# A context vector added to y as it is read from PSUM, and an MLP run earlier in a convolution kernel

## The reference

```python
def _L0_cond_ref(x, c, weight, c_weight, bias):
    out = lax.conv_general_dilated(x, weight, window_strides=(1,), padding=[(4, 4)],
        dimension_numbers=('NCH', 'OIH', 'NCH'), feature_group_count=4)
    ctx = jnp.einsum('nd,od->no', c, c_weight)
    return out + ctx[:, :, None] + bias[None, :, None]
def _L1_cond_ref(x, embedding, W0, b0, W1, b1, W2, b2, weight, bias_k):
    h = jax.nn.gelu(embedding @ W0 + b0, approximate=False)
    h = jax.nn.gelu(h @ W1 + b1, approximate=False)
    att = jax.nn.softmax(h @ W2 + b2, axis=-1)
    agg_w = jnp.einsum('bk,koi->boi', att, weight[..., 0])
    return jnp.einsum('boi,bih->boh', agg_w, x) + (att @ bias_k)[:, :, None]
x = x + _L0_cond_ref(x, cond_128, L0_cond_weight, L0_cond_c_weight, fside_S_0)
x = x + _L1_cond_ref(x, cond_128, ...)
```

## Time and profile before

| | us |
|---|---|
| median of 3 runs (723.7 to 725.74) | 723.83 |
| the profiled execution | 723.61 |
| its span | 721.8 |
| busy: PE, PEld | 712.1, 701.6 |
| busy: DVE, ACT, POOL | 636.0, 602.8, 38.4 |
| DMA, mean | 246 GB/s |

### The profile page before, as it was taken

One profiled execution on the slowest core, in us unless ns is written; L12 is line 12 of the kernel. 1 busy time (PEld: TensorE's weight loads), 2 busy tenths in 40 slices (PEclk: granted clock), 3 DMA queues, 4 the chain that ended last, 5 costly groups with the idle time before them and its releaser, 6 DMA issues.

```text
span 721.8 us, 29496 instructions
## 1 busy us (share of the span) xinstructions
PE 712.1 (99%) x12419; PEld 701.6 (97%) x12419; DVE 636.0 (88%) x1145; ACT 602.8 (84%) x456; POOL 38.4 (5%) x43
## 2 busy tenths in 40 slices
PE   8999999999999999999999999999999999999996
PEld 6899999999999999999999999999999999999995
DVE  6999889889889989889889898998899898898983
ACT  5989888898888898898898898898898898898833
POOL 2890000000000000000000000000000000000000
PEclk9999999999999999999999999999999999999999
DMA  6447778778778678778778778778778778787657
GB/s 225 156 159 258 269 246 276 259 255 270 236 253 283 216 259 275 217 259 269 247 252 270 232 256 254 249 260 255 237 270 261 232 270 257 234 271 243 199 210 241
DMA packets 66551, 177.56 MB, mean 246 GB/s; under 512 B 7437, under 2 KB 50008, under 8 KB 50264
## 3 DMA queue, kind: packets, MB, share of 16 engines
q1 hardware_dynamic: 57218, 112.96, 51.1%
q10 hardware_dynamic: 9302, 64.14, 23.4%
HBM read 101.57 MB, written 75.50 MB: 245 GB/s over the span
## 4 chain that ended last, share of the span: by engine, by line
PE 96%; DMA 2%; DVE 1%; ACT 0%; SPq 0%; issue 0%; DVEq 0%; ACTq 0%
PE ps L451 72%; PE ps L482 24%; DMA x_in<-in_x_dram 1%; DMA mix_dram<-mix_parts 1%; DMA mix_rep<-mix_dram 0%; DVE y_lo L648 0%; PE ps L415 0%; SPq L305 0%; ACT x_hi L534 0%; DVE mix_odd L749 0%; PE ps L404 0%; PE ps L392 0%; DVE mix_even L749 0%; DVE x_in L793 0%; DVEq L72 0%
## 5 line engine op out<-in xcount | busy, mean ns | idle before, releaser
L451 PE MATMUL ps<-x_hi,cw_hi 32*128 32x512 f32 x3072 | 428.6, 385 | 0.4 <-ACT x_hi L534 0.4
L451 PE MATMUL ps<-x_hi,cw_lo 32*128 32x512 f32 x3072 | 428.0, 384 | 0.0
L530 ACT ACTIVATE x_ph<-x_in 128x2560 f32<-128x2560 f32 x63 | 322.2, 5116 | 1.8 <-DVE x_lo L637 1.8
L451 PEld LDWEIGHTS ps<-x_hi,cw_hi 32*128 32x128 f32 x3072 | 317.4, 183 | 2.2 <-issue 0.8
L451 PEld LDWEIGHTS ps<-x_hi,cw_lo 32*128 32x128 f32 x3072 | 317.2, 183 | 0.9 <-issue 0.2
L451 PE MATMUL ps<-x_lo,cw_hi 32*128 32x512 f32 x3072 | 284.9, 384 | 0.0
L451 PEld LDWEIGHTS ps<-x_lo,cw_hi 32*128 32x128 f32 x3072 | 253.2, 183 | 1.7 <-issue 0.8
L482 PE MATMUL ps<-y_hi,mix_rep 32*128 32x512 f32 x2048 | 225.0, 384 | 1.4 <-DMA mix_rep<-mix_dram 1.4
L556 ACT ACTIVATE z_out<-ps,par 128x1024 f32<-128x1024 f32 x124 | 144.3, 1223 | 72.4 <-PE ps L482 57.2
L648 DVE TENSOR_TENSOR y_lo<-ps,y_hi 128x512 fp32r<-128x512 f32 x256 | 158.9, 682 | 47.0 <-ACT y_hi L543 46.9
L482 PEld LDWEIGHTS ps<-y_hi,mix_rep 32*128 32x128 f32 x2048 | 195.1, 183 | 2.5 <-DMA mix_rep<-mix_dram 1.8
(11 more groups left out here) (88 smaller groups left out, 116.3 us busy)
## 6 DMA issues: line engine op xcount, KB each, us to landing
x_in<-in_x_dram SPq DMA_DIRECT2D x64, 1024.0 KB, 7.7
out_dram<-z_out ACTq DMA_DIRECT2D x61, 1024.0 KB, 7.8
mix_rep<-mix_dram SPq DMA_DIRECT2D x256, 128.0 KB, 2.7
mix_dram<-mix_parts SPq DMA_DIRECT2D x64, 128.0 KB, 4.2
out_dram<-z_out SPq DMA_DIRECT2D x2, 1024.0 KB, 3.9
out_dram<-x_in SPq DMA_DIRECT2D x2, 512.0 KB, 3.5
z_out<-in_L_cond_weight_dram SPq DMA_DIRECT2D x1, 512.0 KB, 3.9
cw_nat<-in_L_cond_weight_dram SPq DMA_DIRECT2D x1, 144.0 KB, 2.3
```

Source lines behind the costliest of these rows:

```text
L451: mm = pe.matmul(y_at(s)[:, g, :], w[rows, m, :], x_at(xx[buf(s)], rows, m), start=i == 0, stop=i == CONV - 1)
L530: nc.scalar.activation(x_ph[buf(s)][:, :, :, :], by_lane(x_in[buf(s)]), ACT.Copy).then_inc(x_split_ph, 1)
```

## The change

The context is added to y when it is read. `ctx_all` [128, 64, 4] holds, for each sample and group, the context's 32 values repeated on all four row groups; `spread_context` makes it with four products (`to_rows`, four identities side by side, built by VectorE at the start), in place of the eight of `context_mixed`. For each sample VectorE copies four columns of it to `ctx_now`; `y_hi` becomes an activation Identity with a column bias, and `y_lo` becomes (y + column) - `y_hi` in one three-operand instruction. `finish_table` has two instructions instead of three.

The small network is moved forward: w0 is issued ahead of b0 and b1, the first layer stands ahead of the convolution, second and third layer at steps 6 and 12, the transpositions at 14. Phases 0 and 1 of sample 0 are VectorE's, 2 and 3 ScalarE's, phase 3 behind the first GELU. On VectorE the softmax stands ahead of the second half of x_lo.

At the end, each row group of samples 62 and 63 waits for its own copy (`mix_late`), and SP issues the copies of 62 ahead of the store of 63.

```diff
@@ -157,7 +157,9 @@
 ctx_c = sb("ctx_c", [P, NS])
-agg_b = sb("agg_b", [P, NS])
+ctx_all = sb("ctx_all", [P, NS, G])
+ctx_now = [sb(f"ctx_now{k}", [P, G]) for k in range(U)]
+to_rows = sb("to_rows", [P, PH, Q])
@@ -227,6 +232,10 @@
     return isinstance(s[0], int) and number(s) == b
+def is_late(s):
+    return is_sample(s, NS - 2) or is_sample(s, NS - 1)
@@ -303,7 +312,8 @@
             sp.dma_start(rep_at(s)[Q * r:Q * r + Q, :, :, :].bitcast(F32).rearrange("c g h o -> c g (h o)"),
-                         mix_dram[b].rearrange("(g c) h o -> c g (h o)", g=G)).then_inc(mix_loaded[b], DMA)
+                         mix_dram[b].rearrange("(g c) h o -> c g (h o)", g=G)
+                         ).then_inc(mix_late[b][r] if is_late(s) else mix_loaded[b], DMA)
@@ -328,8 +338,8 @@
         if is_sample(s, NS - 1):
+            load_mix(after(s, -1))
             store_mix(s)
-            load_mix(after(s, -1))
@@ -375,7 +385,7 @@
         pe.wait_ge(first_loaded, DMA)
-        pe.wait_ge(cond_copied, 2)
+        pe.wait_ge(cond_copied, 1)
@@ -408,14 +418,18 @@
         pe.matmul(ps[:, 4, 0:NS], ctxw_t[:, :], cond_t[:, :], start=True, stop=True).then_inc(ctx_mm, 1)
-    def context_mixed():
+    def spread_context():
...
         pe.wait_ge(ctx_made, 1)
-        for k in range(NK):
-            mm = pe.matmul(ps[:, 6, k * NS:(k + 1) * NS], mixw_t[:, k, :], ctx_c[:, :], start=True, stop=True)
-        mm.then_inc(ctx_mix_mm, 1)
-
-    between = {16: first_layer, 18: second_layer, 20: third_layer, 21: turn_mixw, 24: context, 26: attention, 31: context_mixed}
+        pe.wait_ge(table_made, 1)
+        pe.wait_ge(rows_made, G)
+        for g in range(G):
+            rows = slice(Q * g, Q * g + Q)
+            mm = pe.matmul(ps[:, 4 + g, 0:NS], to_rows[rows, :, :].rearrange("c r o -> c (r o)"), ctx_c[rows, :],
+                           start=True, stop=True)
+        mm.then_inc(ctx_spread, 1)
+    between = {6: second_layer, 12: third_layer, 14: turn_mixw, 24: context, 27: attention, 31: spread_context}
@@ -425,7 +439,7 @@
                 if is_sample(s, 0):
-                    pe.wait_ge(x_phase_by_act, 1)
+                    pe.wait_ge(x_phase_by_dve, 1)
@@ -437,9 +451,9 @@
         if g == 0 and i == 4 and is_sample(s, 0):
-            pe.wait_ge(x_phase_by_dve, 1)
+            pe.wait_ge(x_phase_by_dve, 2)
         if g == 0 and i == 8 and is_sample(s, 0):
-            pe.wait_ge(x_phase_by_act, 2)
+            pe.wait_ge(x_phase_by_act, 1)
@@ -459,7 +473,9 @@
         if i == 0:
-            if r == 0:
+            if is_late(s):
+                pe.wait_ge(mix_late[buf(s)][r], DMA)
+            elif r == 0:
@@ -511,10 +527,12 @@
     pe.wait_ge(cond_loaded, DMA)
-    pe.transpose(ps[:, 4, 0:NS], cond_nat[:, :], ident[0:NS, 0:NS])
+    pe.transpose(ps[:, 4, 0:NS], cond_nat[:, :], ident[0:NS, 0:NS]).then_inc(cond_turned, 1)
+    keep_warm(1)
+    first_layer()
...
     pe.transpose(ps[:, 4, P:P + 3], bias_rows[:, :], ident[0:3, 0:3]).then_inc(cond_turned, 1)
-    keep_warm(3)
+    keep_warm(1)
@@ -540,7 +558,9 @@
             at_least(act, z_ready, done(s, PH, lag=-U))
-        nc.scalar.activation(y_hi[s[1]][:, g, :], y_at(s)[:, g, :], ACT.Copy).then_inc(y_hi_made, 1)
+            act.wait_ge(ctx_now_made, done(s))
+        nc.scalar.activation(y_hi[s[1]][:, g, :], y_at(s)[:, g, :], ACT.Identity,
+                             bias=ctx_now[s[1]][:, g:g + 1]).then_inc(y_hi_made, 1)
@@ -571,9 +591,9 @@
         (cond_nat[:, :], cond[:, :], cond_loaded),
+        (w0_sb[:, :], w0[:, :], first_loaded),
...
         (bias_rows[2:3, :], b1.rearrange("(a c) -> a c", a=1), biases_loaded),
-        (w0_sb[:, :], w0[:, :], first_loaded),
@@ -586,11 +606,11 @@
     act.wait_ge(x_loaded[0], DMA)
-    round_phase(0).then_inc(x_phase_by_act, 1)
...
     nc.scalar.activation(h1[:, :], ps[:, 5, 0:NS], ACT.Gelu, bias=cols[:, 1:2]).then_inc(mlp_act, 1)
+    round_phase(3).then_inc(x_hi_made, 1)
@@ -645,11 +665,25 @@
             at_least(dve, z_ready, done(s, PH, lag=-U))
-        nc.vector.tensor_tensor(y_lo[s[1]][:, g, :], y_at(s)[:, g, :], y_hi[s[1]][:, g, :].bitcast(F32),
-                                ALU.subtract).then_inc(y_lo_made, 1)
+            dve.wait_ge(ctx_now_made, done(s))
+        nc.vector.scalar_tensor_tensor(y_lo[s[1]][:, g, :], y_at(s)[:, g, :], ctx_now[s[1]][:, g:g + 1],
+                                       y_hi[s[1]][:, g, :].bitcast(F32),
+                                       ALU.add, ALU.subtract).then_inc(y_lo_made, 1)
+    def take_context(s):
+        if not exists(s):
+            return
+        nc.vector.tensor_copy(ctx_now[s[1]][:, :], ctx_all[:, number(s), :]).then_inc(ctx_now_made, 1)
...
     nc.vector.memset(y_hi[U - 1][:, 0, :].bitcast(F32), 1.0).then_inc(zeros_made, 1)
+    dve.wait_ge(ident_made, 2)
+    for g in range(G):
+        rows = slice(Q * g, Q * g + Q)
+        nc.vector.tensor_copy(to_rows[rows, :, :], ident[rows, rows].unsqueeze(1).broadcast_to([Q, PH, Q])
+                              ).then_inc(rows_made, 1)
@@ -660,9 +694,9 @@
     nc.vector.tensor_copy(cond_t[:, :], ps[:, 4, 0:NS]).then_inc(cond_copied, 1)
-    nc.vector.tensor_copy(cols[:, :], ps[:, 4, P:P + 3]).then_inc(cond_copied, 1)
@@ -676,28 +710,29 @@
     dve.wait_ge(x_loaded[0], DMA)
+    round_phase(0).then_inc(x_phase_by_dve, 1)
     round_phase(1).then_inc(x_phase_by_dve, 1)
-    round_phase(3).then_inc(x_hi_made, 1)
-    dve.wait_ge(x_phase_by_act, 1)
-    dve.wait_ge(x_phase_by_dve, 1)
+    dve.wait_ge(cond_turned, 2)
+    nc.vector.tensor_copy(cols[:, :], ps[:, 4, P:P + 3]).then_inc(cond_copied, 1)
+    dve.wait_ge(x_phase_by_dve, 2)
     rest_half(0)
-    dve.wait_ge(x_phase_by_act, 2)
-    dve.wait_ge(x_hi_made, 1)
-    rest_half(1).then_inc(x_lo_made, 1)
-
...
     nc.vector.tensor_scalar(ntop[:, :], top[:, :], -1.0, None, ALU.mult).then_inc(soft, 1)
-    dve.wait_ge(cond_turned, 2)
-    nc.vector.tensor_copy(ctxw_t[:, :], ps[:, 4, P:2 * P]).then_inc(cond_copied, 1)
-    nc.vector.tensor_copy(mixb_t[:, :], ps[:, 4, 3 * P:3 * P + NK]).then_inc(cond_copied, 1)
...
     nc.vector.tensor_scalar(att[:, :], expd[:, :], inv[:, 0:1], None, ALU.mult).then_inc(soft, 1)
+    dve.wait_ge(x_phase_by_act, 1)
+    dve.wait_ge(x_hi_made, 1)
+    rest_half(1).then_inc(x_lo_made, 1)
+    dve.wait_ge(cond_turned, 3)
+    nc.vector.tensor_copy(ctxw_t[:, :], ps[:, 4, P:2 * P]).then_inc(cond_copied, 1)
+    nc.vector.tensor_copy(mixb_t[:, :], ps[:, 4, 3 * P:3 * P + NK]).then_inc(cond_copied, 1)
@@ -710,21 +745,19 @@
     round_x((0, 1))
-    dve.wait_ge(ctx_mix_mm, 1)
-    dve.wait_ge(cond_copied, 4)
-    nc.vector.tensor_tensor(aggb_prod, ps[:, 6, :].rearrange("p (k s) -> p s k", k=NK),
-                            mixb_t[:, :].unsqueeze(1).broadcast_to([P, NS, NK]),
-                            ALU.add).then_inc(table_made, 1)
+    dve.wait_ge(ctx_spread, 1)
+    nc.vector.tensor_copy(ctx_all[:, :, :].rearrange("p s g -> p g s"), ps[:, 4:8, 0:NS]).then_inc(table_made, 1)
+    dve.wait_ge(table_made, 2)
+    take_context((0, 0))
...
     def finish_table():
-        dve.wait_ge(table_made, 2)
-        nc.vector.tensor_tensor(aggb_prod, aggb_prod, table[:, :, 0:NK], ALU.mult).then_inc(table_made, 1)
+        dve.wait_ge(cond_copied, 4)
+        nc.vector.tensor_tensor(aggb_prod, mixb_t[:, :].unsqueeze(1).broadcast_to([P, NS, NK]),
+                                table[:, :, 0:NK], ALU.mult).then_inc(table_made, 1)
         dve.wait_ge(table_made, 3)
-        nc.vector.tensor_reduce(agg_b[:, :], aggb_prod, AX.X, ALU.add).then_inc(table_made, 1)
-        dve.wait_ge(table_made, 4)
-        nc.vector.tensor_tensor(table[:, :, NK:NK + 1].rearrange("p s a -> p (s a)"), agg_b[:, :],
-                                ctx_c[:, :], ALU.add).then_inc(table_made, 1)
+        nc.vector.tensor_reduce(table[:, :, NK:NK + 1].rearrange("p s a -> p (s a)"), aggb_prod,
+                                AX.X, ALU.add).then_inc(table_made, 1)
@@ -769,6 +802,7 @@
             rest_y(s, g)
+        take_context(after(s, 1))
@@ -845,7 +879,7 @@
         if is_sample(s, 0):
-            pool.wait_ge(table_made, 5)
+            pool.wait_ge(table_made, 4)
```

5 lines of the change are left out of this document (4 added, 1 removed).

## The result

Median of six launches each: before 723.64 us (723.08 to 725.74), changed 728.0 us (725.91 to 729.82); ratio 1.0048, 95% interval 1.0029 to 1.0067. The change is slower (the interval lies above 1), and 728.0 lies above the forecast of 723.9 us and its upper end of 726.0. The profiled launch is the fastest of the six, 725.91, with a span of 724.1; it holds 2.3 of the 4.4 us between the medians.

What follows compares the result with a forecast made beforehand. The prediction took TensorE to bound the loop, with VectorE's chain and the copies also limiting the ends. From 723.61 us, loop 0.0, ramp +0.3 and tail +0.1 gave 724.0, or 724.2 against the median; it said 723.9, range 721.5 to 726.0.

Steps and rivals of the forecast that it cites:

- Loop, 0.0: Middle samples: added work on VectorE (0.46 us a sample) and ScalarE (0.36) stays covered by TensorE, costing 0.0.
- rival 3: Loop: the three-operand subtraction runs at half rate, 2.15 us more a sample, 96 us in all, time 820; chance 2%.
- Start, -0.4: Start of the ramp: the convolution begins at 8.3 us instead of 8.69, -0.4 (bounds -0.65 and 0).
- the stand before sample 2: Ramp: TensorE's wait for VectorE's x_hi of sample 2; the forecast's sum gave it no term of its own.
- Split of sample 2 from 20.8, x_hi ready at 32.25, sample 2 at 32.3: Ramp: a later load holds ScalarE's split of sample 2, so sample 2 begins at 32.3 instead of 32.43, -0.1.
- Rival 1: Ramp and tail: TensorE's own work is the limit at both ends, 3.6 us are kept, time 720.2; chance 13%.
- rival 2: Ramp: the load of sample 2 lands late; taking 6.8 us it adds 2.1, time 726.1; chance 11%.
- Ramp behind it, +0.3: Samples 2 to 4: VectorE's gapless chain grows by 0.7, GpSimd gives back 0.3; TensorE +0.3 late (bounds -0.5 and +0.9).
- the early places of the small products: Ramp: first layer ahead of the convolution saves an estimated 0.5 us of insertion; third layer, ahead of step 12, ends near 12.1.
- the tail, +0.1: Last samples: matrix 63's later store and first copy cost +0.3 (bounds -0.7 and +1.5); earlier output leaves +0.1.

Runs made afterwards that it cites:

- e9: The changed kernel launched again, unedited: median 727.2 us, ratio 1.0028 to 1.0079.
- e12: The changed kernel without its tail edits (context and small-network edits only): median 726.1 us, ratio 1.0023 to 1.0068.
- e14: The changed kernel with SP's old order in the tail, waits by row group kept: median 725.6 us, ratio 1.0018 to 1.0057.
- e3: The kernel before with only the small network moved forward, including the new start and VectorE order: median 723.8 us, ratio 0.9990 to 1.0034.
- e6: e3 with three warming products instead of one ahead of the convolution: median 724.2 us, ratio 0.9997 to 1.0031.
- e16: The kernel before with only the network's small products moved to steps 4, 8, 12 and 14: median 723.4 us, ratio 0.9995 to 1.0044.
- e18: e3 run once more as the control for its two halves: median 724.8 us, ratio 0.9994 to 1.0036.
- e15: e3 with second and third layer back at steps 16 and 18, transpositions at 20: median 728.7 us, ratio 1.0038 to 1.0077.
- e1: The changed kernel with eight unused warming products in TensorE's wait before sample 2: median 727.8 us, ratio 1.0036 to 1.0094.
- e7: e1 with three warming products instead of one ahead of the convolution: median 726.9 us, ratio 1.0046 to 1.0111.
- e2: The kernel before with only the context edits (column bias, third operand, spread, copies): median 724.3 us, ratio 0.9987 to 1.0025.
- e17: The kernel before with only the new start (first layer ahead of the convolution, w0 earlier, phases swapped, one warming product): median 722.8 us, ratio 0.9973 to 1.0005.
- e10: The changed kernel with the eight products of context_mixed put back, results unused: median 727.0 us, ratio 1.0038 to 1.0087.
- e13: The kernel before with only the waits by row group for samples 62 and 63, SP's order as before: median 722.7 us, ratio 0.9972 to 1.0005.
- e4: The kernel before with only the tail edits (row waits and SP's new order): median 725.2 us, ratio 0.9994 to 1.0024.
- e11: The changed kernel without the small-network edits (context and tail edits only): median 725.0 us, ratio 1.0001 to 1.0027.
- e8: The changed kernel with VectorE's second half of x_lo ahead of the softmax again: median 726.5 us, ratio 1.0008 to 1.0059.

## Why the prediction was wrong, step by step

- **Loop, 0.0: right.** 631.04 us in both. y_lo costs 62 ns more (forecast 55), y_hi 91 (forecast 90; 599 and 690). The Trainium skill (ScalarE: Activation LUTs, What ACT_TABLE_LOAD costs) says about 93 for a column operand: the trace agrees. The Trainium skill's halved rate (Vector Engine (DVE) Microarchitecture Reference, section 7), stated for two SBUF sources, doesn't appear here with one source in PSUM: 744 against 682. So rival 3 fell.
- **Start, -0.4: right.** 8.18 against 8.3. Sample 1 came at 21.66 instead of the 22.65 forecast, since x_hi took 1.48 and not 2.37; it had slack, but came a microsecond sooner to the stand before sample 2.
- **Split of sample 2 from 20.8, x_hi ready at 32.25, sample 2 at 32.3: right** (20.96, 32.24, 32.30), the last hundredths by luck: x_hi of sample 2 began 0.26 later than forecast (30.76 for 30.5) and took 1.48 instead of 1.75. Rival 1 fell with it, and rival 2, since the load landed in time.
- **Ramp behind it, +0.3: right where the clock holds** (+0.48 in e9).
- **What failed first: the stand was priced at nothing.** By the forecast's own times TensorE is through with sample 1 at 22.65 + 36 x 0.228 = 30.9 and sample 2 begins at 32.3: a stand of 1.4, which entered the sum as lost gain only. It was 2.14, and cost 1.65 in the profiled launch, 1.6 in e12 and in e14, nothing in e9. The nearest row was the stand of 1.40 in the tail, behind which the clock held at 1.00; as an upper bound it should have been a few microseconds at half pace all the same.
- **What failed second: the early places of the small products** were counted as free or a gain. They bring the long launches of e3, e6, e16 and e18. Of the changed kernel's own launches three of e9's eight are of the kind with the clock reading full (730.33 to 730.84, clock 0.997 to 0.999), and four of the first six of the other kind (727.78 to 729.82, clock 0.991 to 0.993). By the arithmetic of e15, 0.991 to 0.993 is 7 to 10 us at half pace and 3.6 to 5 us lost, which takes 724.0 to 727.6 to 729: about what those four took. Where in them the clock was low is not shown, as none was profiled. It can't be laid on the stand alone: launches with such a clock come in e16, which has neither the stand nor any other edit (three of twelve, 728.1 to 728.4), and in e1 and e7, where the stand is filled (six of 23).
- **What failed third: the tail, +0.1, was mis-sized.** The store took 2.51, as forecast (2.8), and the first copy of matrix 63 2.4 (forecast 2.7). Counted from the first product of sample 63, the first product with matrix 63 came 0.7 sooner than before, not 0.3 later. But the sum went by the first copy alone, and the third and fourth took 3.72 and 3.59: row group by row group TensorE waits for them, and its last product ends 0.6 later than before. The tail as a whole lost 0.53, against 0.32 in e9. Of this the context part has its share (e2 and e12: 26.1 and 26.0 with the tail of before); against e12 the tail's two edits come out even in these two launches, where the row waits alone would have gained 1.6 (e14 against e12). In every profile with the new order of SP the tail is 1.2 us or more longer than with the row waits alone.

The changed kernel's whole loss isn't one thing. The early places are shown by counts of launches (e16 against before, and against e17), SP's order by the tails of all profiles. The stand is shown in single launches only: three of four profiles with it lost the clock, none of the three with it filled or short. How the 4.4 us of the medians divide among the three is open: filling the stand (e1, e7, e10) doesn't lower the median, and launches of the changed kernel and its variants reach 730 to 735, above the 729.2 to 729.8 of the network's part alone.

The best kernels are two halves of the change: e17 at 722.8 and e13 at 722.7, each 0.9989 of before, with an interval that just reaches 1 (1.0005), so the gain isn't clear of noise. Both profiles are 1.0 to 1.3 us shorter than that of before, at places that don't touch each other (ramp and tail). The two together weren't tried.

## What to carry to other kernels

Taking work off TensorE ahead of a wait for another engine gains nothing (e10), and the stand that it leaves can be followed by microseconds at half the clock: price a new stand of one or two microseconds with products at the lower level, as an upper bound. Where a change touches the start, look at the spread of a dozen launches and at their clocks, since the fastest launch, the profiled one here, shows the least of the loss. Split a change with several edits early: the start and the row waits look like gains of a microsecond each in their profiles, hidden here by the other edits. When a wait is split into four, size the last of the four transfers, not the first.

## What the hardware showed that was not expected

- The half pace at the start (0.62 us a product instead of 0.38, until 11 us in e4 and e11, until 21 us in e3, e6 and e18) is not in the granted clock of the stretches, which reads 1.00.
- A stand of 1.9 to 2.2 us before sample 2 brought the clock to 0.50 for about 3 us in three profiles and not in a fourth; one of 2.4 in e8 to 0.52 to 0.63 for 4; one of 1.28 in e15 for ten. Behind single stands of 1.3 to 1.6 us in the tail (before, e10, e12, e15 and others) it held.
- The copy of 128x4 to `ctx_now` cost VectorE 0.63 in the ramp, beside GpSimd at work, and 0.16 at the median of its 64 times; GpSimd's subtraction took 2.93 beside a busy VectorE and 0.46 beside an idle one (e8).
- Of four copies issued one behind the other, the first landed 2.4 us after its issue and the third 3.7, where the output's transfers had begun in between (changed kernel, tail).
